# A graph network's edge table in slots that begin at each block's first edge

## The reference

```
h = relu(layernorm(x)); z = layernorm(h) * g + b
q, k, v = z @ Wq + bq, z @ Wk + bk, z @ Wv + bv          # 8 heads of 64
scores = einsum('ehd,ehd->eh', q[dst], k[src]) / 8 + bias   # per edge and head
p = exp(scores - segment_max(scores, dst))
out = segment_sum(p / segment_sum(p, dst) * v[src], dst) @ Wo + bo
```

## Time and profile before

| | |
|---|---|
| median of 3 runs | 394.1 us (393.75 to 395.66) |
| the profiled execution | 394.1 us, its span 394.1 us |
| busy | PE 374.8 us (95%), DVE 312.1 us (79%), ACT 171.6 us (44%) |
| start to the first pair product | 22.06 us |
| pair loop, until its last product | 22.06 to 108.3 us |

### The profile page before, as it was taken

The page is one execution under the profiler, slowest core; times in us unless marked ns, Lnnn a source line. Parts: engine busy times, 40 slices in busy tenths (PEclk is TensorE's granted clock), DMA queues, the critical chain, the costliest instruction groups (busy, mean ns, idle before and its releaser), DMA issues.

```text
span 394.1 us, 5108 instructions
## 1 busy us (share of the span) xinstructions
PE 374.8 (95%) x1786; PEld 282.2 (72%) x1786; DVE 312.1 (79%) x660; ACT 171.6 (44%) x287; POOL 4.2 (1%) x19
## 2 busy tenths in 40 slices
PE   2989999999999999999999999999999999999994
PEld 1545566666657888887678788887588878787773
DVE  5889999999848789897868976698875788388236
ACT  5664666563044234244559533262363530145410
POOL 4000000000000000000000000000000000000000
PEclk9999999999999999999999999999999999999988
DMA  7602444343135000068200512200600050000002
GB/s 238 250 1 69 152 154 141 105 153 112 52 112 183 1 2 0 2 215 315 111 2 1 172 43 101 114 0 0 211 4 0 2 180 33 2 0 0 2 12 94
DMA packets 16360, 32.92 MB, mean 84 GB/s; under 512 B 1360, under 2 KB 1488, under 8 KB 16336
## 3 DMA queue, kind: packets, MB, share of 16 engines
q1 hardware_dynamic: 15744, 32.25, 23.9%
q10 hardware_dynamic: 592, 0.36, 0.3%
HBM read 21.07 MB, written 1.05 MB: 56 GB/s over the span
## 4 chain that ended last, share of the span: by engine, by line
PE 77%; DVE 14%; ACT 4%; issue 2%; DMA 1%; DVEq 0%; ACTq 0%
PE acc L1395 11%; PE bank L1377 10%; PE bank L1480 7%; PE bank L1270 6%; PE bank L1271 6%; PE bank L1251 4%; PE acc L1251 4%; PE acc L1271 4%; PE acc L1270 4%; PE bank L1465 3%; PE acc L1451 3%; DVE big_rounded L652 2%; PE acc L1228 2%; PE bank L1228 2%; PE acc L1545 2%
## 5 line engine op out<-in xcount | busy, mean ns | idle before, releaser
L1395 PE MATMUL acc<-wide_rounded,c_rounded 128*126 128x512 f32 x200 | 59.5, 439 | 0.7 <-ACT acc L464 0.7
L1395 PEld LDWEIGHTS acc<-wide_rounded,c_rounded 128*126 128x126 f32 x200 | 36.9, 186 | 19.8 <-issue 13.0
L792 DVE TENSOR_SCALAR wide_rounded<-iota_f,picked 128x512 fp32r<-128x512 f32 x100 | 42.2, 480 | 1.5 <-issue 1.1
L483 ACT COPY z_sb<-acc 126x512 f32<-126x512 f32 x37 | 21.6, 585 | 42.0 <-PE acc L1395 33.3
L507 ACT ACTIVATE wide<-wide,low_col 128x512 f32<-128x512 f32 x32 | 21.3, 715 | 32.9 <-DVE low_col L905 32.8
L1480 PEld LDWEIGHTS bank<-v_sb,big 128*128 128x128 f32 x256 | 29.7, 192 | 4.7 <-issue 4.0
L625 DVE TENSOR_TENSOR wslot_rounded<-wslot,wide_rounded 128x512 fp32r<-128x512 f32 x24 | 16.2, 687 | 21.2 <-ACT wslot L377 21.2
L1480 PE MATMUL bank<-v_sb,big 128*128 128x65 f32 x256 | 31.6, 277 | 0.0
L798 DVE TENSOR_TENSOR c_rounded<-row_bc,wslot_rounded 128x1008 fp32r<-128x1008 bf16 x25 | 30.0, 1201 | 0.0
L1377 PE MATMUL bank<-t_sb,wslot 128*128 128x512 f32 x64 | 29.5, 594 | 0.5 <-ACT t_sb L459 0.5
L652 DVE TENSOR_TENSOR big_rounded<-big,big_rounded 128x1024 fp32r<-128x1024 f32 x24 | 29.1, 1221 | 0.5
(11 more groups left out here) (312 smaller groups left out, 769.6 us busy)
## 6 DMA issues: line engine op xcount, KB each, us to landing
big<-z_sb SPq DMA_DIRECT2D x36, 252.0 KB
big<-in_w SPq DMA_DIRECT2D x4, 2048.0 KB, 7.8
x_sb<-in_x SPq DMA_DIRECT2D x8, 256.0 KB, 4.6
big<-in_w_3t SPq DMA_DIRECT2D x2, 1024.0 KB, 6.7
row_bc<-in_rows SPq DMA_DIRECT2D x7, 256.0 KB, 6.4
wslot<-in_wq SPq DMA_DIRECT2D x1, 1024.0 KB, 8.9
wslot<-in_wk SPq DMA_DIRECT2D x1, 1024.0 KB, 10.7
wslot<-in_wv SPq DMA_DIRECT2D x1, 1024.0 KB, 12.8
```

The costliest lines, as they stand in the source:

```text
L483: nc.scalar.copy(stage[0:BROWS, b % STAGES, :], a).then_inc(S["staged"], 1)
L792: nc.vector.tensor_scalar(hot_ring[:, u, k, :], iota_f[:, :], picked[:, 0, s0 + k:s0 + k + 1], None, ALU.is_equal)
L1395: last = nc.tensor.matmul(to, st_ring[:, u, 2 * k + a, :, :].rearrange("p w k -> p (w k)"), hot_ring[:, u, k, :], start=False, stop=False, ...
```

## The change

A slot no longer follows the tiles. It is a run of 128 edges that begins at a block's first edge and goes on by 128, over the border of two tiles if need be; a block has as many slots as its edges fill. The program has 84 slots (`SLOTS`), 20 fixed groups and the loop. For this input, the blocks' edge counts give 81 slots in all, and before the (tile, block) pairs gave exactly 100. In the order of work the blocks take 1, 1, 1, 2, 1, 1, 2, 1, 2, 2, 1, 1, 1, 1, 2, 2, 2, 1 slots, then mostly 2, and at the end 3, 3, 3, 3, 4, 5, 11; before they took 1, then nineteen times 2, then 2 or 3, and at the end 4, 4, 4, 6, 11.

Since a slot may lie in two tiles, each lane needs its edge from the first or the second of them: the picks are made twice (336 columns for 200), and DVE mixes the two with `copy_predicated` by a mask of lanes (`second`). DVE and PE get a longer chain to find each block's first and last edge (`outer`, `apart`, `xy`, `flag`, `count`, `start`), and POOL six more iotas. The layer norms' moments go between the steps of the table. The products of the bias weights (`first_weights`) and six steps of QKV now stand ahead of the pair loop, and after each of the 19 first groups stand two steps. The two first tiles of `t_sb` are scaled by DVE. All four accumulators are cleared by PE, where ACT cleared two. The DMAs of the blocks, the three stage buffers, the reading of ends and the rest of the kernel are as before.

```
-SLOTS = 100
+SLOTS = 84
...
-ENDS, PICK, NEEDS = 130, 200, 400
+SPAN, ENDS, FIRST, LANE, NEEDS = 80, 84, 128, 216, 304
+EARLY = 6
+FAR = 1000
...
+        in_whole = c1[:, :, :].rearrange("p t n -> p (t n)")[:, GROUP * 2 * BROWS:][:, 0:H * SLOTS].rearrange(
+            "p (h s) -> p h s", h=H)
+        chunk_whole = wslot[:, 3, :, :].rearrange("p t n -> p (t n)")[:, SLOTS * 2 * KW:][:, 0:H * GROUP].rearrange(
+            "p (h s) -> p h s", h=H)
...
-        qkv_group = [g for g, steps in enumerate([7, 4, 3] + [2] * 10 + [1] * 10 + [0]) for _ in range(steps)]
-
-        Z_BANKS = (3, 0, 4, 5)
+        qkv_group = [-1] * EARLY + [g for g, steps in enumerate([2] * (NG - 2) + [0, 0]) for _ in range(steps)]
...
+        qkv_bank = [bank[b] for b in (6, 7, 4, 5) + 2 * (4, 5, 6, 7)]
...
+            nc.gpsimd.iota(lane_c, [[0, 1]], base=0, channel_multiplier=1,
+                           allow_small_or_imprecise_dtypes=True).then_inc(S["tables"], 1)
+            nc.gpsimd.iota(no_lane_c, [[0, 1]], base=0, channel_multiplier=-1,
+                           allow_small_or_imprecise_dtypes=True).then_inc(S["tables"], 1)
+            nc.gpsimd.iota(lanes[:, 0, :], [[-1, P]], base=P, channel_multiplier=0,
+                           allow_small_or_imprecise_dtypes=True).then_inc(S["tables"], 1)
+            nc.gpsimd.iota(lanes[:, 1, :], [[1, P]], base=1, channel_multiplier=0,
+                           allow_small_or_imprecise_dtypes=True).then_inc(S["tables"], 1)
+            for a in range(2):
+                pool.wait_ge(S["tables"], 8 + a)
+                nc.gpsimd.iota(tile_at[a * ET:(a + 1) * ET, :, :], [[-1, 2], [-1, SLOTS]], base=-FAR,
+                               channel_multiplier=1, allow_small_or_imprecise_dtypes=True).then_inc(S["tables"], 1)
...
-            act.wait_ge(S["weights_mm"], 1)
-            for q in range(2):
-                from_pe = bank[6 + q][:, 0:4 * SLOTS].rearrange("p (h s) -> p s h", h=4)
-                nc.scalar.copy(wp[:, 0:SLOTS, 0, 4 * q:4 * q + 4], from_pe).then_inc(S["w_hi"], 1)
             ln_stds(1)
             act.wait_ge(S["ln_coef"], 2 * NT)
             for t in (2, 3):
                 nc.scalar.activation(z_sb[:, t, :], h_sb[:, t, :], ACT.Identity, bias=shift[:, t:t + 1],
                                      scale=rstd[:, t:t + 1]).then_inc(S["z_scalar"], 1)
+            act.wait_ge(S["bias_low"], 1)
+            for h in range(HP):
...
+            for t in (2, 3):
                 act.wait_ge(S["turned"], t + 1)
-                nc.scalar.activation(t_sb[:, t, :], bank[Z_BANKS[t]][:, :], ACT.Identity, bias=colp("ln1_b", t),
-                                     scale=colp("ln1_g", t)).then_inc(S["t_ready"], 1)
-
-            def clear(b):
-
-                nc.scalar.copy(bank[b][0:BROWS, :], zero_c[0:BROWS, :].broadcast_to([BROWS, N])
-                               ).then_inc(S["evacuated"], 1)
...
+            by_two = in_whole.rearrange("p (h a) s -> p h a s", a=2)
+            x_moments(2)
+            dve.wait_ge(S["ranks_mm"], 1)
+            nc.vector.scalar_tensor_tensor(out=outer, in0=bank[4][0:ET, 0:2 * NBK].rearrange("p (b n) -> p b n", b=2),
+                                           scalar=1.0, in1=meets.unsqueeze(1).broadcast_to([ET, 2, NBK]),
+                                           op0=ALU.is_equal, op1=ALU.mult).then_inc(S["outer_ready"], 1)
+            x_moments(3)
+            dve.wait_ge(S["outer_mm"], 1)
+            dve.wait_ge(S["tables"], 10)
+            dve.wait_ge(S["lows_ready"], 1)
+            of = bank[5][0:NBK, 0:2 * P].rearrange("p (b l) -> p b l", b=2)
+            link(nc.vector.scalar_tensor_tensor(out=apart, in0=of, scalar=low_c, in1=lanes, op0=ALU.is_ge, op1=ALU.mult))
+            link(nc.vector.scalar_tensor_tensor(out=apart, in0=of, scalar=high_c, in1=apart, op0=ALU.is_le, op1=ALU.mult))
+            link(nc.vector.tensor_reduce(xy, apart, AX.X, ALU.max))
+            link(nc.vector.tensor_scalar(flag, xy[:, 1:2], xy[:, 0:1], float(P), ALU.add, ALU.is_gt))
+            nc.vector.tensor_tensor(count, bank[4][0:NBK, SPAN:SPAN + 1], flag, ALU.add).then_inc(S["counts_ready"], 1)
+            ln_coefs(0)
+            dve.wait_ge(S["src_in"], 16)
+            mark(nc.vector.tensor_copy(src_f, idx_src))
+            dve.wait_ge(S["bias_in"], 16)
+            nc.vector.tensor_reduce(bmax[:, 0:HP], att_b, AX.X, ALU.max).then_inc(S["bias_top"], 1)
+            dve.wait_ge(S["ends_mm"], 1)
+            link(nc.vector.tensor_copy(ends[:, :], bank[4][0:NBK, ENDS:ENDS + 2]))
+            mark(nc.vector.scalar_tensor_tensor(out=start, in0=bank[4][0:NBK, SPAN + 1:SPAN + 2], scalar=-float(FAR),
+                                                in1=ends[:, 0:1], op0=ALU.add, op1=ALU.subtract))
+            mark(nc.vector.tensor_copy(ends_row[:, 0:NBK], bank[4][0:1, ENDS + 2:ENDS + 2 + NBK]))
             settle()
             dve.wait_ge(S["pick_zeros"], 1)
             slot_table(0, 0, whole)
-            dve.wait_ge(S["bias_spread"], 1)
-            nc.vector.tensor_scalar(bmax_all[:, 0:HP], bank[6][:, P:P + HP], -1.0, W_SHIFT, ALU.mult, ALU.add
-                                    ).then_inc(S["bias_low"], 1)
-            x_moments(2)
-            slot_picks(0, 0, whole)
-            x_moments(3)
-            slot_columns(0, 0, whole)
...
             for t in (0, 1):
                 ln_plain(1, t, h_sb)
+            dve.wait_ge(S["bias_spread"], 1)
+            nc.vector.tensor_scalar(bmax_all[:, 0:HP], bank[6][:, 0:HP], -1.0, W_SHIFT, ALU.mult, ALU.add
+                                    ).then_inc(S["bias_low"], 1)
+            step(4, slot_masks(early), False)
+            dve.wait_ge(S["tables"], 13 + NT)
+            one_hots(0, 0, (0, 1))
+            dve.wait_ge(S["cols_in"], 16)
+            for t in (0, 1):
+                dve.wait_ge(S["turned"], t + 1)
+                nc.vector.tensor_scalar(t_sb[:, t, :], bank[t][:, :], colp("ln1_g", t), colp("ln1_b", t),
+                                        ALU.mult, ALU.add).then_inc(S["t_vector"], 1)
+            one_hots(0, 0, (2, 3))
+            dve.wait_ge(S["weights_mm"], 1)
+            dve.wait_ge(S["w_whole"], 1)
+            nc.vector.copy_predicated(by_two, with_second(whole, HP, 2), from_tables(1)).then_inc(S["w_mixed"], 1)
+            dve.wait_ge(S["w_mixed"], 1)
+            dve.sem_inc(S["weights_read"], 1)
+            rounded(4, early, by_two[:, :, :, early])
             left_sides(0, 0)
-            slot_weights(5, later)
-            dve.sem_inc(S["weights_read"], 1)
-            build(1, 1, GROUP)
+            one_hots(1, GROUP)
+            dve.wait_ge(S["w_hi"], 1)
+            step(7, nc.vector.tensor_tensor(wp[:, later, 1, 0:H], in_whole[:, :, later].rearrange("p h s -> p s h"),
+                                            wp[:, later, 0, 0:H].bitcast(F32), ALU.subtract))
+            left_sides(1, GROUP)
...
+            def weights_in_two(base, c, of, first, other):
+
+                step(base + 1, nc.vector.tensor_copy(of, first))
+                held_wait(base)
+                step(base + 2, nc.vector.copy_predicated(of, with_second(c, HP, 2), other))
+                rounded(base + 2, c, of)
+
+            def rounded(base, c, of):
+
+                step(base + 1, nc.vector.tensor_copy(wp[:, c, 0, 0:H], of.rearrange("p h a s -> p s (h a)")))
+                step(base + 2, nc.vector.tensor_tensor(wp[:, c, 1, 0:H], of.rearrange("p h a s -> p s (h a)"),
+                                                       wp[:, c, 0, 0:H].bitcast(F32), ALU.subtract))
...
+            def first_weights():
+
                 pe.wait_ge(S["weights_exp"], HP)
...
+                    pe.wait_ge(*((S["t_vector"], h + 1) if h < 2 else (S["t_ready"], 2 * h - 2)))
+                    last = nc.tensor.matmul(bank[h][:, 0:4 * SLOTS], att_b[:, h, :], pick, start=True, stop=True)
...
+            all_slots = slice(0, SLOTS)
             bias_turned()
+            slot_tables(0, all_slots)
+            slot_edges(0, all_slots)
             bias_spread()
-            pe.wait_ge(S["tables"], 6)
-            pe.wait_ge(S["lows_ready"], 1)
-            pair_table(0, slice(0, SLOTS))
-            zeros((1, 2)).then_inc(S["pair_mm"], 1)
             pe.wait_ge(S["rows_ready"], 1)
             held = choices(0, 2 * GROUP)
-            keep_warm(3, 8)
-            pe.wait_ge(S["round_steps"], 2)
+            keep_warm(7, 4)
             for i, t in enumerate((0, 2, 1, 3)):
                 pe.wait_ge(*((S["z_ready"], t + 1) if t < 2 else (S["z_scalar"], t - 1)))
                 for c in range(NT):
-                    last = nc.tensor.transpose(tile(bank[Z_BANKS[c]], t), tile(z_sb[:, t, :], c), ident[:, :])
+                    last = nc.tensor.transpose(tile(bank[c], t), tile(z_sb[:, t, :], c), ident[:, :])
                     if i == NT - 1:
                         last.then_inc(S["turned"], 1)
+            pe.wait_ge(S["bias_low"], 1)
+            qkv_step(0)
```

(18 more changed lines are left out.)

275 lines of the change are left out of this document (143 added, 132 removed).

## The result

The changed kernel takes 405.94 us (median of 4 runs, 404.46 to 406.78), the one before 394.0 beside it: a ratio of 1.029, 95% interval 1.025 to 1.033. It is slower, as forecast, but by 11.9 us where I had 6, and 0.9 us outside my range. One number of mine was wrong at the start: a run is some 1.5 us longer than its span (406.24 and 404.8 in the profiled execution of after). Before's profiled execution has a span of 394.1, so its time was the 395.66 at the top of the list, and I took span and time for one number. The runs of before fall in two clusters, spans near 392.3 and near 393.9; the profiled one, with its late fall of the clock, is of the longer. The profile of after has such a late fall too (the clock at 0.50 for 3.4 us from 387.3 on), so I compare the two spans: 394.1 and 404.8, +10.7.

What follows compares the result with a forecast made beforehand. PE and DVE were both taken as full in the pair loop, PE the tighter after the change. Late banks put the last product 5.3 us later, the tail adds 0.75: 394.1 + 5.3 + 0.75 = 400.1; range 393.5 to 405.

Steps and rivals of the forecast that it cites:

- the tail: Behind the pair loop: four more picks and predicated copies with their links add 0.75 us; nothing changes behind that.
- The saving on PE: In the pair loop: four groups fewer at 1.85 us of pair products each save PE 7.4 us.
- the recurrence: Early pair loop: block n needs block n-4's bank; PE waits at slots 5 to 7, 9, 16 to 18, 10.3 us in all.
- ends at 34.75: Ahead of the loop: DVE's small table work, on which ACT's first copy waits, ends at 34.75 us, against 26.81 before.
- the bias products: Ahead of the loop: four PE products of 336 columns take 2.25 us at the loop's rate, done at 26.7 with the wait.
- the norm's scaling: Ahead of the loop: the second layer norm's scaling comes at 20.0 to 21.1 us, where it was at 19.68 to 20.68.
- The subtraction: DVE, ahead of the loop after the first one-hots: the rest's subtraction takes 0.75 us; two of 368 columns took 1.00.
- Groups 3.58 us apart: Sign in the pair loop: from 60 us on, groups with two QKV steps follow each other every 3.58 us.
- The POOL term: Start of the kernel: a copy held until POOL's six more iotas are done ends 1.25 us later, delaying the chain.
- rival 1: Clock: PE's low level slows bias products, the QKV step ahead or the loop; with two of three 403 to 405; chance 0.16.
- Rival 2: Same: block 0's DMA no longer holds ACT, only ACT's late start counts; time 394; chance 0.11.
- rival 3: Faster: banks never hold PE in the loop; time 390; chance 0.13.

Runs made afterwards that it cites:

- all four edits: Changed kernel with a fourth stage place, ends_ready moved early, extra TensorE products ahead of the transposes, QKV steps spread 4, 5, 2, ..., 1: 392.29 us.
- the 4, 4, 2 kernel: The kernel with all four edits, its QKV steps spread as 4, 4, thirteen times 2, four times 1: 392.48 us, ratio 0.995 to the one before.
- four places: The changed kernel with four stage buffers instead of three (STAGES = 4): 402.07 us.
- two edits: Four stage buffers and ends_ready early: in the changed kernel 397.61 us; in the kernel before 395.35 us against 393.98.

## Why the forecast was right, and where it was not

**Right:** PE goes to the early slots before ACT has freed their banks. The fourth copy comes 9.06 us behind the first (9.07 forecast), slots 5 and 9 wait, the tail is +0.7 (0.75), nothing changes behind it. PE stands idle 9.1 us in the loop, 7.4 of them for ACT's clears, where I had 10.3. The saving on PE, 4 x 1.85, fits too: with all four edits the loop takes 74.2 us with one wait of 1.79 in it, for the 71.7 I had without waits. The longest waits in the loop, 3.06 and 2.62 us, stand where the recurrence put them, at 3.1 us later times (41.06 for 37.95, 50.13 for 47.0).

**The step that failed** is "ends at 34.75" in the part on the way to the loop. They came at 37.64, and the 2.9 us go through the recurrence undiminished (first copy 39.63 for 36.75); the mechanism held, and what I had too short is the way to the ends. 2.1 of the 2.9 us stand at the end of the bias products, 28.8 for 26.7. Of its terms the norm's scaling was 0.6 early (19.40 for 20.0). The transposes had no term of their own: I had carried z to 21.55 and the bias products to 26.7 over table load and exponentials, which ended at 23.50, but DVE's and ACT's scalings of t waited for transposes that took 3.62 us for 1.94 before, and the QKV step ahead of the bias products waited for these. The bias products then took 2.42 us (2.25 forecast). The subtraction, 0.75 forecast, took 1.26: 608 elements read across heads, where the row I used had runs of four. ACT's rounding of the same shape took 1.24. The predicated copy cost 0.91 (0.85). First pair product: 33.62 for 31.7. In the one profile of the new way in which the transposes took 1.91 us, that of the 4, 4, 2 kernel, it starts at 31.42 (they also begin 0.7 earlier there). That the transposes are the term I had left out rests on this and on DVE's wait of 2.88 us for them.

**"Groups 3.58 us apart"** failed in two places. The waits at slots 16 to 18, which I had from 54.9 on, came from 58.74 on, and behind them ACT's clears hold PE no more, as forecast. But groups 6 and 8 start 4.41 and 4.71 us behind theirs where I had 3.58. From group 5 to group 9 that is 15.65 us for 14.3; with 3.45 us late at group 5 (63.25 for 59.8) it makes up 4.8 of the 5.3 us at the last product (118.9 for 113.6). The left sides of both groups had been built some 4 us before (63.7 and 71.4), so it was not DVE. The view names "issue", and PE's program reads the block numbers of the next eight slots just ahead of groups 6 and 8; that this reading is the cause is argued, not tested. In the kernel with all four edits PE is idle 1.79 us in the whole loop (72.38 us busy of 74.17), and that is the one wait shown above.

**The POOL term** of 1.25 us was wrong. POOL's six more iotas run beside DVE, and the copy it should have held took 0.21 us at 2.24 (the timeline of both):

```profile
2.24 0.21 DVE L703 COPY slot<-rcnt_sb 128x84 f32<-128x84 f32 x1 [1.18 <-POOL z_sb L368]
2.26 0.12 POOL L372 IOTA small<- 128x1 f32 x1
...
2.45 0.24 POOL L376 IOTA row_bc<- 37x128 f32 x1
```

I had called one row the trace's agreement with the Trainium skill (GPSIMD Engine Reference, Key points) on the shared interfaces, and made of it that the copy waits until POOL is done. It does not: POOL goes on here until 6.2 us. Whether the interfaces are shared these rows do not settle. Before, the copy of 0.75 us ran beside POOL's memsets of 200 and 100 columns; here it ran beside iotas of one column, and the memsets come after 3.6 us.

**The rivals.** The clock fell as rival 1 had it, for 3.41 us from 42.59 on, and four matmuls took 2.71 us for 1.88. (It was low at the transposes too, which the rival did not name; the bias products, which it did, ran at the full level.) It cost nothing there: PE was back at 47.51 and waited until 50.13 all the same. Rival 2 (the landing does not hold ACT) is refuted by the row of 48.69 and by four places, rival 3 by the first copy at 39.63. Rival 3's price was not far off as a bound: with the waits gone 392.3, against its 390.

**What the change is worth.** Take the kernel with all four edits. Its first pair product starts at 33.23, 11.2 us later than 22.06; the six QKV steps ahead of it give 6 x 0.87 = 5.2 back, and 16 slots 7.4. That makes -1.4, and its last product ends at 107.4 for 108.7. (Its wait of 1.79 us has its match in waits of 0.7 and 0.5 at the start of before's loop.) The tail takes 0.7 of it: the turning of the counts starts at 113.91 for 114.47. The span is 2.5 us shorter all the same, and 1.9 of that lie behind this point, where before's clock fell from 377.25 on the earlier trace rows and here, at the same distance, it did not (busy time by stretch):

```profile
376.70:380.10 3.40, 3.40 (x17) 2.81 (x16) 1.78 (x5) 0.30 (x1) 0.00 (x0) 1.00 0.00 0
```

So of the 1.7 us between the medians these two profiles explain some 0.6. The late fall does not explain the rest: the median runs of both kernels had a mean clock of 0.999, where the profiled one of before, with the fall, has 0.992. The profiled execution of this kernel is the slowest of its six, with the clock's rise in the midst of the transposes (23.3); that the others rose earlier and won the rest there fits the 4, 4, 2 kernel's profile, but no profile of them shows it. It stays open.

## What to carry to other kernels

An engine can be 95% busy and still be saved only by the order of its work: look which filler (here 14 QKV steps after three groups) lies over a late release before you move it away. When a change makes the consumer reach a ring sooner, recompute when each slot of the ring comes free, and start the releasing engine's chain (here four tiny operations) as early as its data allow. A repair is only worth what the bound of that kernel lets through: two edits gave 8.3 us after the change and nothing before it.
